# A conditioned residual stack of two grouped convolutions and two dynamic mixes: new prologue, and x split straight from its natural order

## The reference

```python
def _L0_cond_ref(x, c, weight, c_weight, bias):          # layers 0 and 3
    out = lax.conv_general_dilated(x, weight, window_strides=(1,), padding=[(4, 4)],
                                   dimension_numbers=('NCH', 'OIH', 'NCH'), feature_group_count=4)
    return out + jnp.einsum('nd,od->no', c, c_weight)[:, :, None] + bias[None, :, None]
def _L1_cond_ref(x, embedding, W0, b0, W1, b1, W2, b2, weight, bias_k):   # layers 1 and 2
    h = jax.nn.gelu(embedding @ W0 + b0, approximate=False)
    h = jax.nn.gelu(h @ W1 + b1, approximate=False)
    att = jax.nn.softmax((h @ W2 + b2) / 1.0, axis=-1)
    agg_w = jnp.einsum('bk,koi->boi', att, weight[..., 0])
    return jnp.einsum('boi,bih->boh', agg_w, x) + (att @ bias_k)[:, :, None]
x = x + L0(x); x = x + L1(x); x = x + L2(x); x = x + L3(x)
```

## Time and profile before

| what | value |
|---|---|
| median of 3 runs | 716.52 us (715.67 to 716.72) |
| profiled execution, its own time | 715.86 us |
| its span, first to last instruction | 714.1 us |
| mean granted TensorE clock | 0.967 |
| PE busy | 664.8 us (93%) |
| DVE busy | 484.8 us (68%) |
| ACT busy | 256.5 us (36%) |
| POOL busy | 253.5 us (36%) |
| chain that ended last | PE 91%, DVE 3%, DMA 2% |

### The profile page before, as it was taken

One profiled execution on the slowest core, in us unless ns is written; L12 is line 12 of the kernel. 1 busy time (PEld: TensorE's weight loads), 2 busy tenths in 40 slices (PEclk: granted clock), 3 DMA queues, 4 the chain that ended last, 5 costly groups with the idle time before them and its releaser, 6 DMA issues.

```text
span 714.1 us, 24424 instructions
## 1 busy us (share of the span) xinstructions
PE 664.8 (93%) x11104; PEld 650.9 (91%) x11104; DVE 484.8 (68%) x941; ACT 256.5 (36%) x319; POOL 253.5 (36%) x94
## 2 busy tenths in 40 slices
PE   4846999999999999999999999999999999999970
PEld 4645889999999999999999999999999999999960
DVE  5378677767676667776777776787777777777221
ACT  3303433343334443434333444343443344432211
POOL 7022233343344444334334444433433444422220
PEclk9957999999999999999999999999999999999986
DMA  8131478889988888889998888888999888666666
GB/s 274 61 90 31 114 184 194 182 155 206 175 181 187 192 192 190 189 166 176 206 174 182 187 192 191 190 185 163 180 206 180 171 192 194 134 131 128 109 120 152
DMA packets 50238, 119.72 MB, mean 168 GB/s; under 512 B 5865, under 2 KB 25369, under 8 KB 42265
## 3 DMA queue, kind: packets, MB, share of 16 engines
q1 hardware_dynamic: 48592, 118.66, 77.7%
q10 hardware_dynamic: 1352, 0.57, 0.3%
q0 software_dynamic: 256, 0.01, 0.0%
HBM read 35.33 MB, written 33.55 MB: 96 GB/s over the span
## 4 chain that ended last, share of the span: by engine, by line
PE 91%; DVE 3%; DMA 2%; ACT 1%; issue 1%; ACTq 0%; SPq 0%; DVEq 0%
PE ps L683 77%; PE ps L724 12%; DMA out_planes<-in_L_cond_c_weight 1%; DMA out_planes<-out_taps 1%; DVE out_planes L561 1%; DVE acc L540 1%; PE ps L711 1%; PE ps L753 1%; DVE y_lo L503 0%; DVE z_lo L513 0%; DVE mat2T L540 0%; ACT out_sb L411 0%; PE ps L778 0%; DVE mat L540 0%; DVE taps_lo L569 0%
## 5 line engine op out<-in xcount | busy, mean ns | idle before, releaser
L337 POOL COPY out_sb<-out_planes 128x2048 f32<-128x2048 f32 x31 | 122.1, 3939 | 301.2 <-DMA out_planes<-out_taps 301.2
L683 PE MATMUL ps<-z_hi,taps_hi 32*128 32x512 f32 x1536 | 203.8, 402 | 3.6 <-DVE z_lo L513 3.6
L683 PE MATMUL ps<-x_hi,taps_hi 32*128 32x512 f32 x1536 | 202.2, 397 | 1.0 <-DVE prod L553 1.0
L683 PE MATMUL ps<-z_hi,taps_lo 32*128 32x512 f32 x1536 | 201.2, 394 | 0.5 <-issue 0.5
L683 PE MATMUL ps<-x_lo,taps_hi 32*128 32x512 f32 x1536 | 200.9, 394 | 0.0
L683 PE MATMUL ps<-x_hi,taps_lo 32*128 32x512 f32 x1536 | 200.7, 393 | 0.0
L683 PE MATMUL ps<-z_lo,taps_hi 32*128 32x512 f32 x1536 | 200.3, 393 | 0.0
L330 POOL COPY x_planes<-x_in 128x2048 f32<-128x2048 f32 x31 | 120.3, 3881 | 138.9 <-DVE x_lo L496 135.8
L388 ACT ACTIVATE y_hi<-ps,bias_tab 128x512 fp32r<-128x512 f32 x128 | 77.6, 690 | 213.5 <-PE ps L683 213.5
L513 DVE SCALAR_TENSOR_TENSOR z_lo<-ps,bias_tab,z_hi 128x1024 fp32r<-128x1024 f32 x64 | 79.2, 1280 | 74.9 <-ACT z_hi L398 74.9
L683 PEld LDWEIGHTS ps<-z_hi,taps_hi 32*128 32x128 f32 x1536 | 120.8, 186 | 6.1 <-DVE z_lo L513 4.0
(11 more groups left out here) (102 smaller groups left out, 566.2 us busy)
## 6 DMA issues: line engine op xcount, KB each, us to landing
out_planes<-out_taps SPq DMA_DIRECT2D x128, 256.0 KB, 7.4
x_in<-in_x SPq DMA_DIRECT2D x31, 1024.0 KB, 11.0
out<-out_sb SPq DMA_DIRECT2D x31, 1024.0 KB, 4.2
mix_w<-prod SPq DMA_DIRECT2D x128, 128.0 KB, 4.5
x_in<-in_x SPq DMA_DIRECT2D x2, 512.0 KB, 6.1
out<-out_sb SPq DMA_DIRECT2D x2, 512.0 KB, 3.1
out_taps<-in_L_cond_weight SPq DMA_DIRECT2D x1, 512.0 KB, 9.5
mix_w<-in_L_cond_weight SPq DMA_DIRECT2D x1, 512.0 KB, 13.2
```

Of the source, the lines that this page charges most:

```text
L337: pool.tensor_copy(out_sb[t.par(d)][:, :].rearrange("c (s p) -> c p s", p=PH), out_planes[:, :, :])\
L683: tile = pe.matmul(ps[:, first_bank + g, :], w[rows(g), d, :], a[rows(g), d % PH, d // PH:d // PH + S], start=(n == 0), stop=(n == TURNS - 1))
```

## The change

DVE now turns the tap weights with its 32x32 block transpose (`turn_taps`), without PE and PSUM; `fold`, which holds the one for the residual, comes from POOL. The tile `x_planes` is gone with all of its copies: ACT and DVE read x with a stride of 4 elements from `x_in` (`planes`). The 4 bias vectors of the MLP are loaded as rows and turned by PE. A second table load of ACT, for Exp, is put ahead of its use. `conv_turns` takes all 12 shifts of hi by hi first, then taps-lo by x-hi, then taps-hi by x-lo, in every convolution, and waits for `x_lo` only at turn 24. The first convolution of image 0 is cut into pieces with the small products between them, that of image 1 starts before the mix of image 0, and SP loads x after `spread_mix_w` in each step, and waits for `x_lo` there.

```diff
--- before.py
+++ after.py
...
+        def planes(buf, s):
+
+            return buf[:, PH * s.start:PH * s.stop].rearrange("c (s p) -> c p s", p=PH)
...
-                sp.wait_ge(x_planed, b - 1)
+                wait(sp, x_lo_done, b - 1)
...
-                if t.has(4):
-                    load_x(t, 4)
...
                     spread_mix_w(t, 1)
+                if t.has(4):
+                    load_x(t, 4)
...
             load_x(zero, 2)
+            spread_mix_w(zero, 0)
+            spread_mix_w(zero, 1)
             load_x(zero, 3)
-            spread_mix_w(zero, 0)
-            for t in ALL:
+            load_x(zero, 4)
+            for t in ALL[1:]:
...
+            for g in range(G):
+                pool.wait_ge(fold_done, g + 1)
+                pool.affine_select(out=fold[:, :], in_=fold[:, :], compare_op=ALU.not_equal, fill=1.0, base=-GC * g,
...
-            plane_x(Step(0, 0), 1)
...
-                act.wait_ge(x_planed, b + 1)
+                act.wait_ge(x_loaded[p], DMA * (t.pair(d) + p))
...
-                act.activation(x_hi[p][:, :, 1:S + 1], x_planes[:, :, :], ACT.Copy).then_inc(x_hi_done, 1)
+                act.activation(x_hi[p][:, :, 1:S + 1], planes(x_in[p], slice(0, S)), ACT.Copy).then_inc(x_hi_done, 1)
...
+                act.wait_ge(taps_raw_step[l], 2)
+                act.activation(phase_columns(taps_hi, l, p), taps_raw[l][:, :, :], ACT.Copy)\
...
+                if t.at(1):
+                    high_x(t, 2)
...
+            for l, m in enumerate((mix1, mix2)):
+                for n in range(2):
+                    act.dma_start(mlp_rows[2 * l + n:2 * l + n + 1, :], m[1 + 2 * n].rearrange("(a c) -> a c", a=1))\
+                       .then_inc(mlp_rows_in, DMA)
+            for l, m in enumerate((mix1, mix2)):
+                act.dma_start(mlp_w[l][0], m[0]).then_inc(hidden_w_in[0], DMA)
...
+            for l, m in enumerate((mix1, mix2)):
+                act.dma_start(mlp_w[l][1], m[2]).then_inc(hidden_w_in[1], DMA)
+            for p in range(PH):
...
+                act.dma_start(key_b[l], m[5].rearrange("(a k) -> a k", a=1)).then_inc(key_b_in, DMA)
+
+            def high_x0(h):
...
+                act.activation(x_hi[0][:, :, 1 + half(h).start:1 + half(h).stop], planes(x_in[0], half(h)), ACT.Copy)\
...
+
+            act.wait_ge(halo_done, HALOS)
+            high_x0(0)
+            act.dma_start(side_groups, side.rearrange("(g o) -> g o", g=G)).then_inc(side_in, DMA)
+            for l, w in enumerate((ctx0_w, ctx3_w)):
+                act.dma_start(ctx_in[l], w).then_inc(ctx_w_in[l], DMA)
+            high_x0(1)
+            gelus(0)
             for p in range(PH):
...
+                taps_high(1, p)
             gelus(1)
+            act.activation(soft[0:1, 41:42], ones[0:1, 0:1], ACT.Exp).then_inc(exp_tables, 1)
+            act.wait_ge(max_done, 2)
+            for l in range(2):
...
-            act.wait_ge(bias_tab_done, 2)
-            zero = Step(0, 0)
-            high_y(zero)
             mix2_transposed(0)
             mix2_transposed(1)
+            zero = Step(0, 0)
             high_x(zero, 1)
-            for p in range(PH):
-                taps_high(1, p)
-            for t in ALL:
+            act.wait_ge(bias_tab_done, 2)
+            high_y(zero)
+            high_z(zero)
+            high_y(Step(0, 1))
+            high_x(zero, 2)
...
-                dve.tensor_tensor(out=x_lo[p][:, :, 1:S + 1], in0=x_planes[:, :, :],
+                dve.tensor_tensor(out=x_lo[p][:, :, 1:S + 1], in0=planes(x_in[p], slice(0, S)),
...
-            def tap_blocks(l):
+            def turn_taps(l):
+
                 dve.wait_ge(conv_w_in[l], DMA)
-                wait(dve, taps_psum, l)
-                for g in range(G):
...
-                dve.tensor_tensor(out=blocks[:, PAD, :], in0=blocks[:, PAD, :], in1=ident[:, :], op=ALU.add)\
-                   .then_inc(blocks_step, 1)
+                dve.transpose(taps_raw[l][:, :, :], conv_in[l].rearrange("o c t -> o t c")).then_inc(taps_raw_step[l], 1)
+                dve.wait_ge(fold_done, 1 + G)
+                dve.wait_ge(taps_raw_step[l], 1)
+                dve.tensor_tensor(out=taps_raw[l][:, PAD, :], in0=taps_raw[l][:, PAD, :], in1=fold[:, :], op=ALU.add)\
+                   .then_inc(taps_raw_step[l], 1)
...
+                if t.at(1):
+                    low_y(t)
...
-                if not t.at(0) and t.has(0):
+                if t.has(0) and not t.at(1):
...
-                if t.has(2):
+                if t.has(2) and not t.at(1):
...
                     evac_out(t, -1)
+                if t.at(1):
...
+                if t.at(1):
+                    low_x(t, 2)
...
+            turn_taps(0)
+            dve.wait_ge(taps_zeroed, 4)
             for p in range(PH):
                 taps_low(0, p)
-            dve.wait_ge(halo_done, HALOS)
-            dve.wait_ge(x_planed, 1)
-            for h in range(2):
...
+            dve.wait_ge(condT_psum, 2)
+            dve.tensor_copy(mlp_col[:, :], ps[:, 6, 0:N + 4]).then_inc(condT_done, 1)
+            low_x0(0)
+            turn_taps(1)
+            low_x0(1)
+            dve.wait_ge(taps_zeroed, 8)
+            for p in range(PH):
+                taps_low(1, p)
...
-            dve.wait_ge(bias_psum, 1)
-            dve.wait_ge(bias_tab_zeroed, 1)
-            bias_table(0)
-            bias_table(1)
...
-            low_y(zero)
...
-            dve.wait_ge(mix2T_done, 2)
             mix_matrices(zero, 0)
...
+            dve.wait_ge(bias_psum, 1)
+            dve.wait_ge(bias_tab_zeroed, 1)
...
+            dve.wait_ge(mixed_psum, 1)
...
             split_product(zero, 0)
-            dve.wait_ge(x_planed, 2)
-            low_x(zero, 1)
-            tap_blocks(1)
-            dve.wait_ge(mixed_psum, 1)
...
-            for p in range(PH):
-                taps_low(1, p)
+            mix_matrices(zero, 1)
             dve.wait_ge(bias_tab_done, 3)
-            for t in ALL:
+            low_y(zero)
+            split_product(zero, 1)
+            low_x(zero, 1)
+            low_z(zero)
+            for t in ALL[1:]:
                 one(t)
...
-                    d, k = n // 3, n % 3
-                    w, a = ((taps_hi[l], hi), (taps_hi[l], lo), (taps_lo[l], hi))[k]
+                    k, d = n // SHIFTS, n % SHIFTS
+                    w, a = ((taps_hi[l], hi), (taps_lo[l], hi), (taps_hi[l], lo))[k]
...
                 b = t.i
                 if turns[0] == 0:
-                    pe.wait_ge(x_lo_done, b + 1)
+                    pe.wait_ge(x_hi_done, b + 1)
                     wait(pe, out_act, 2 * (b - 1))
                     wait(pe, out_dve, 2 * (b - 1))
-                conv_turns(bank(t, 0), 0, x_hi[t.par(0)], x_lo[t.par(0)], conv0_done, turns)
+                for low in (False, True):
+                    part = [n for n in turns if (n >= 2 * SHIFTS) == low]
+                    if low and part and part[0] == 2 * SHIFTS:
+                        pe.wait_ge(x_lo_done, b + 1)
+                    conv_turns(bank(t, 0), 0, x_hi[t.par(0)], x_lo[t.par(0)], conv0_done, part)
...
-            tap_matmuls(0)
+            pe.wait_ge(mlp_rows_in, 4 * DMA)
+            pe.transpose(ps[:, 6, N:N + 4], mlp_rows, ident[0:4, 0:4]).then_inc(condT_psum, 1)
             hidden(0)
+            pe.wait_ge(taps_hi_done[0], PH)
+            conv0(zero, range(4))
+            hidden(1)
+            conv0(zero, range(4, 9))
...
                 pe.wait_ge(ctx_w_in[l], DMA)
                 pe.transpose(ps[:, 7, 128 * l:128 * l + 128], ctx_in[l], ident[:, :]).then_inc(ctxT_psum, 1)
-            hidden(1)
-            logits()
+            conv0(zero, range(9, SHIFTS))
             pe.wait_ge(taps_lo_done[0], PH)
-            conv0(zero, range(MID))
...
+            mix2_transposes(0)
...
-            conv0(zero, range(MID, TURNS))
-            mix2_transposes(0)
-            pe.wait_ge(att_tab_done, 1)
+            conv0(zero, range(16, 20))
             mix2_transposes(1)
+            conv0(zero, range(20, 24))
...
-            pe.wait_ge(mix2T_done, 2)
-            pe.wait_ge(agg_done, 1)
+            conv_biases()
+            conv0(zero, range(24, 32))
+            mixed_bias()
             product(zero, 0)
-            mixed_bias()
-            tap_matmuls(1)
-            for t in ALL[:2 * LOOP[0]]:
-                one(t)
+            conv0(zero, range(32, TURNS))
+
+            pe.wait_ge(bias_tab_done, 2)
+            pe.wait_ge(mixed_step, 1)
+            pe.wait_ge(prod_summed, 1)
+            conv0(first, range(20))
+            product(zero, 1)
+            conv0(first, range(20, 2 * SHIFTS))
+            mix(zero)
+            conv0(first, range(2 * SHIFTS, TURNS))
+            pe.wait_ge(taps_lo_done[1], PH)
+            one(first)
```

182 lines of the change are left out of this document (69 added, 113 removed).

## The result

The changed kernel takes 773.03 us (median of 4 runs, 770.49 to 774.66) against 716.25 us of before in the same series (715.67 to 716.72): 1.079 times the time, with an interval of 1.0757 to 1.0823. The prediction, 693.5 us in a range of 687 to 701, is wrong in sign.

The account below looks back on a forecast made before the run. PE was taken to bound the steady steps at 19.82 us, leaving gains only before 86.87 us. 86.87 - 61.3 - 2.8 = 22.8 us gained, from 715.86 to 693.1, stated as 693.5, range 687 to 701.

Parts of the forecast that it names:

- Steady steps: Steps after the prologue: PE's work the same, `out_taps` with 1.3 us of slack, moved load harmless; cost nothing, 19.8 us each.
- `x_lo`: DVE's split of x in each steady step: stride free, 2.28 us, ending at 144.1 instead of 143.6.
- slower `x_lo`: Rival, steady steps: DVE pays the stride, 4.7 us, PE waits 0.9 us in each of 29 steps; 698 to 721, chance 0.06.
- Prologue: Stretch up to the end of image 1's mix, where PE waits: that end moves from 86.87 to 61.3 us.
- X: Moment in the prologue when `x_hi` is ready for the first convolution: 12.3 us, bounds 10.5 to 14.
- M: Prologue moment when PE ends the mixed biases: X plus 19.7 us of turns and small work, 32.0 us.
- E: End of image 1's mix: M + 28.1 = 60.1 us, plus 1.2 for a possible clock fall, 61.3.
- new wait for `y_lo`: Between M and E, PE stands at the product for image 1 until DVE ends `y_lo`: 3.2 us.
- Whether the clock falls in such a hole: In PE's 3.2 us hole the clock may fall or not, costing 2.5 us if so; half, 1.2, taken.
- The next step: Step behind image 1's mix: PE waits 2.8 us for `y_lo`, behind DVE's extra `x_lo` and the matrices for image 3.
- The tail: Stretch behind the mix of image 30 at 661.78 us: has holes, but its lists are untouched, so no change.

Follow-up runs that it names:

- b1: Kernel before, with only SP's order of the changed kernel (spread, load of x four images ahead, next re-laying); 778.97 us against 716.5.
- a1: Changed kernel with SP's load of x three images ahead, directly behind the re-laying DMAs; 719.06 us, ratio 1.0029.
- a4: Changed kernel in its own order, loading only an eighth of x's columns from image 5 on; 717.45 us.
- p2: a1 with extra single instructions of 1024 columns in its tail, contiguous, strided and in DVE/POOL pairs; its total time was not to be read.
- a3: a1 with all splits of x reading contiguously, phases not sorted out; 699.57 us.
- b2: Kernel before with strided splits of x for images 1 to 31, no POOL copies, and the order of a1; 725.86 us, ratio 1.0137.
- g6: g4 with convolution turns put between PE's two conv biases and between the mixed biases; 698.21 us, ratio 0.9759.
- g4: Changed kernel, load three ahead behind re-laying, `out_taps` ahead of `x_lo`, MLP weights issued earlier, `x_lo` of image 3 moved to step 2; 698.45 us, ratio 0.9758.
- a5: Changed kernel with SP's order re-laying, spread, load four ahead, store; 803.89 us.

## Why the prediction was wrong, point by point

**Steady steps: the step that failed.** "The moved load of x goes ahead of the re-laying DMAs in the queue and may delay them by 3 or 4 us, against 7 us of slack until ACT overwrites the tile." The delay was sized about right: issuing the load takes 0.6 us ahead of the re-laying, and by the medians the re-laying lands after 13.6 us instead of 11.2, 3.0 us in all. The slack was not 7 us. That is the distance from landing (275.70 in the step shown of before) to the next write of `out_taps` by ACT (282.84); but the landing is also followed by the weave, the store, the spread and the next re-laying, each held by SP's order, and in that circle there was 0.6 us of air. 3.0 less 0.6 is 2.4 us, and by that a step grew, from 19.8 to 22.2. Shown by b1 (the order alone, +62.5), a1 (the order back, -54) and a4 (the bytes of the load taken away, landing at 11.4).

**`x_lo`: mis-sized.** 2.28 assumed, 3.87 measured. The reason given was L604, 1113 ns, "the speed without a stride". p2 shows that a contiguous copy by DVE takes 0.69: L604 had paid already. The rival "slower `x_lo`" had the mechanism and put the price at 4.7 us and 0.9 a step, with nothing lost up to 3.8; it is 3.87 and 0.44 (a1 against a3, and b2), hidden in after behind the circle. The rule of two accesses to a line from the Trainium skill, "SBUF — State Buffer", section "Door 1: The DMA port swizzle", which the prediction set aside for DVE, was right for both engines.

**Prologue: right in kind, 17.1 us won where 25.6 were foreseen up to mix 1.** The second half of `x_hi` on ACT, and then PE (start, us):

```profile
9.75 2.03 ACT L459 ACTIVATE x_hi<-x_in 128x1024 fp32r<-128x1024 f32 x1
```

```profile
12.83 1.06 PE L794 MATMUL ps<-mlp_col,out_sb 128*128 128x32 f32 x4 [5.67 <-DMA out_sb<-in_L_cond_W]
13.82 2.08 PE L693 MATMUL ps<-x_hi,taps_hi 32*128 32x512 f32 x16
...
35.74 3.62 PE L770 MATMUL ps<-agg,mix_wT 128*128 128x32 f32 x16
...
48.71 0.46 PE L725 MATMUL ps<-mat2T,mat 32*128 32x128 f32 x5 [0.91 <-DVE y_lo L511]
...
85.90 0.81 PE L725 MATMUL ps<-mat2T,mat 32*128 32x128 f32 x8 [3.54 <-DVE y_lo L511]
```

- X: `x_hi` ready at 11.8 (12.3 foreseen), the stride at 2.02 (2.0), the transpose 0.69 (0.7), hidden. But PE started at 13.8: the MLP's first weights, which I had "in time" (3.5 + 7.0 us), landed at 12.8.
- M: 39.4 instead of 32.0. 1.5 of it is the start. The most is a clock that I had not reckoned with: the earlier trace rows show it falling in holes only; here it fell while the trace has PE busy all the time, in a row of small products (L778 and L782).

```profile
30.00:31.00 1.00, 1.00 (x7) 0.88 (x7) 0.96 (x5) 1.00 (x1) 0.00 (x0) 0.85 0.00 0
31.00:32.00 1.00, 1.00 (x6) 0.96 (x5) 0.00 (x0) 0.72 (x1) 0.00 (x0) 0.50 0.03 8
32.00:36.00 4.00, 4.00 (x35) 2.76 (x34) 0.49 (x2) 0.00 (x0) 0.00 (x0) 0.50 0.00 0
...
44.00:45.00 1.00, 1.00 (x20) 0.83 (x16) 1.00 (x5) 0.47 (x1) 0.00 (x0) 0.82 1.13 151
```

  From 30.9 to 39.4 at half speed is by estimate 4.3 us that would not have been there at 1.00. The 1.6 that are left are not settled: small products that took longer than the sum had for them.
- E: 69.8 instead of 61.3, 7.4 of it from M (M to E 30.4, foreseen 28.1 + 1.2). The new wait for `y_lo` was 0.9 us and not 3.2, since PE's turns went at the low clock; with the clock held (g6) it is 3.0. Whether the clock falls in such a hole was rightly left open: in g4, with a wait of 3.0 us as well, it is at 0.50 from 44 us on, in g6 it stays at 1.00. 1.2 us for `x_lo` of image 1 came on top.
- The next step: wait 3.5 us (2.8 foreseen) for the reason foreseen; g4 puts it, somewhat shorter, into the step behind.

**The tail** was called untouched. Its lists are, but the last re-laying is behind the store of the image before, and issued at 753.41, 2.1 us after its data (`out_taps` ends at 751.3): the same circle. That is half of the 4.3 us; the rest was not followed up.

**What the mended versions say of the forecast.** With SP's order and DVE's order mended the kernel is at 698, inside the range. That is another kernel than the one forecast, and its 698 do not make the forecast good; they show that the prologue's gain is real once the steps are back at 19.8.

## What to carry to other kernels

When a transfer is moved in an in-order queue, do not ask how long its neighbours can wait until their own consumer: follow every path from the queue's instruction back to the same queue (landing, copy, store behind it, the next issue), add it up to a circle and compare it with the step. Take the air in that circle from several steps: here the first ones had more than 2 us, the later ones 0.6. A long load belongs behind the short transfers that other engines wait for. Before a price is read from a row as "without a stride", look for a row that has none.

## What the runs showed of the hardware that was not expected

- A stride of 2 in fp32 is free or nearly so (1.23 us on DVE and 1.12 on ACT for 1024 columns, against 1.23 and 1.06 contiguous); one of 4 or 8 costs DVE's subtraction 0.74 to 0.76 us and ACT's copy 0.95 to 0.98, and a second strided stream costs nothing more.
- POOL's copy of 2048 columns and DVE's subtraction from SBUF stretched each other from 3.9 to 7.0 and 7.5 us (a5), and it stretched a cast by DVE of 128 columns from 0.23 to as much as 3.8.
- A load of 1 MB issued just ahead of four transfers of 256 KB put their landing from 11.2 to 13.6 us; with an eighth of its bytes it was 11.4 (a4).
- PE's granted clock fell to 0.50 at 30.8 us in after while PE showed as busy without a gap, in a row of small products, and stayed at 1.00 from 22 to 44 us when large ones were put between them (g6).
